# Sorting token numbers instead of token rows for the routed experts of a two-layer tower

## What is computed

```python
x = take(weight, idx)                         # 2048 rows of 256
x = x + LN(causal_linear_attention(LN(x)))    # layer 0, 16 heads, 16 tiles of 128 rows
x = x + ((LN(x) @ CB.T) * SCB / 127 + bias)
x = performer_block(LN(x), ...)               # layer 1: attention by 64 features, two matrices of 1024
logits = LN(x) @ router_w.T                   # 8 experts
top = argmax(logits); s = sigmoid(max(logits))
h = LN(x) * s                                 # the row that goes to its one expert
routed = (silu(h @ gate[top]) * (h @ up[top])) @ down[top]
shared = (silu(LN(x) @ sg) * (LN(x) @ su)) @ sd
out = x + shared + routed
```

## Time and profile before

| | |
|---|---|
| runs, us | 748.58, 749.82, 751.64; median 749.82 |
| profiled execution | 749.15 us, of it the span from the first to the last instruction 747.3 |
| mean granted TensorE clock | 0.970 |
| busy, share of the span | PE 91%, PEld 75%, DVE 64%, ACT 37%, POOL 27% |
| DMA | 69.81 MB, HBM read 28.74 MB, written 41.10 MB |
| chain that ended last | PE 83%, DVE 6%, issue 3%, the rest 8% |

### The profile page before, as it was taken

One profiled execution on the slowest core, in us unless ns is written; L12 is line 12 of the kernel. 1 busy time (PEld: TensorE's weight loads), 2 busy tenths in 40 slices (PEclk: granted clock), 3 DMA queues, 4 the chain that ended last, 5 costly groups with the idle time before them and its releaser, 6 DMA issues.

```text
span 747.3 us, 15335 instructions
## 1 busy us (share of the span) xinstructions
PE 679.7 (91%) x5738; PEld 563.1 (75%) x5739; DVE 481.6 (64%) x1185; ACT 277.1 (37%) x664; POOL 204.1 (27%) x379
## 2 busy tenths in 40 slices
PE   3838899999999999999999999999997399999995
PEld 2627788988889898989989898888886256565653
DVE  2549688887969788797988879777663422323231
ACT  1114443544344444534444453453442022222220
POOL 4632233313232422323242232422321011111111
PEclk9869999999999999999999999999999699999998
DMA  7999999999999500000000000000015411211110
GB/s 257 323 230 173 168 190 168 177 147 180 166 162 217 210 1 16 16 1 16 1 15 5 13 15 2 15 1 16 16 57 223 138 34 56 64 45 64 63 57 17
DMA packets 30911, 69.81 MB, mean 93 GB/s; under 512 B 3323, under 2 KB 9600, under 8 KB 29440
## 3 DMA queue, kind: packets, MB, share of 16 engines
q1 hardware_dynamic: 27696, 60.53, 37.0%
q0 software_dynamic: 3152, 8.40, 3.8%
HBM read 28.74 MB, written 41.10 MB: 93 GB/s over the span
## 4 chain that ended last, share of the span: by engine, by line
PE 83%; DVE 6%; issue 3%; ACT 2%; POOL 2%; DMA 2%; POOLq 0%; SPq 0%; DVEq 0%; ACTq 0%
PE ps L1030 76%; PE ps L1035 5%; PE ps L1199 2%; DMA H<-table,idx_sb 2%; POOL H L371 2%; ACT qkA L635 1%; DVE stats L659 1%; ACT yTB L625 1%; PE ps L1329 0%; POOL rstd L391 0%; DVE S_sb L725 0%; DMA yA<-sorted_rows 0%; DVE mv L660 0%; DVE kmax L811 0%; PE ps L1170 0%
## 5 line engine op out<-in xcount | busy, mean ns | idle before, releaser
L1030 PEld LDWEIGHTS ps<-yTC,we 128*128 128x128 f32 x1024 | 120.6, 194 | 6.5 <-issue 5.0
L1030 PE MATMUL ps<-yTC,we 128*128 128x128 f32 x1024 | 124.8, 279 | 0.5 <-ACT yTC L579 0.5
L390 POOL TENSOR_TENSOR var_eps<-mv,ln_eps 128x1 f32<-128x1 f32 x112 | 23.9, 213 | 370.4 <-DVE mv L660 370.1
L1030 PE MATMUL ps<-we,yTA 128*128 128x256 f32 (+1 forms) x288 | 97.1, 469 | 1.7 <-ACT yTB L625 1.4
L1030 PEld LDWEIGHTS ps<-we,yTA 128*128 128x128 f32 x288 | 54.6, 200 | 26.0 <-issue 20.9
L1030 PE MATMUL ps<-we,yTB 128*128 128x256 f32 (+1 forms) x216 | 73.1, 469 | 0.7 <-DVE yTB L863 0.6
L391 POOL TENSOR_TENSOR rstd<-var_eps,pow_half 128x1 f32<-128x1 f32 x112 | 66.4, 593 | 8.8
L1030 PE MATMUL ps<-we,ffT 128*128 128x256 f32 x256 | 61.3, 383 | 0.0
L1030 PEld LDWEIGHTS ps<-we,yTB 128*128 128x128 f32 x216 | 38.7, 191 | 23.7 <-issue 21.0
L1030 PEld LDWEIGHTS ps<-we,ffT 128*128 128x128 f32 x256 | 47.2, 190 | 5.6
L472 POOL DMA_INDIRECT out<-tmpA,home x12 | 11.8, 985 | 127.3 <-DVE tmpA L1019 127.3
(11 more groups left out here) (197 smaller groups left out, 1315.2 us busy)
## 6 DMA issues: line engine op xcount, KB each, us to landing
sorted_rows<-pads SPq DMA_DIRECT2D x16, 2052.0 KB, 49.1
we<-w_experts SPq DMA_DIRECT2D x8, 1536.0 KB, 19.5
home<-sorted_rows SPq DMA_DIRECT2D x23, 128.5 KB, 2.1
we<-w_ff SPq DMA_DIRECT2D x2, 1024.0 KB
rows_sb<-rows SPq DMA_DIRECT2D x1, 1664.0 KB, 7.0
yA<-sorted_rows SPq DMA_DIRECT2D x12, 128.0 KB, 2.1
yB<-sorted_rows SPq DMA_DIRECT2D x11, 128.0 KB, 2.1
we<-w_qk SPq DMA_DIRECT2D x2, 512.0 KB, 4.1
```

What stands on the lines that cost most here:

```text
L390: link(pool.tensor_tensor(var_eps[:, k:k + 1], mv[:, k, 1:2], ln_eps[:], ALU.add))
L1030: return pe.matmul(o, a, b, start=start, stop=stop)
```

## The change

The rows are no longer scattered. SP writes the scaled rows (`x_rows`) and the rows with the shared expert's part (`home_rows`) in token order by plain DMAs, with stages `x_out` and `home_out`. Only the tokens' numbers are scattered, 4 bytes each, into `sorted_ids`, which one write of out-of-bounds numbers clears beforehand; the 17 writes of padding rows go. When the table is there, SP loads for each of the 23 sorted tiles its column of 128 numbers (`load_ids`), each with a `value_load` and a DMA, two on one semaphore and 21 on another. The tiles are then fetched by these numbers with indirect DMAs that GpSimd issues (`fetch_x`, `fetch_home`); numbers out of bounds are left out.

The gathers from the table of rows are spread: three at the start, ahead of the constants' memsets, and one in each step behind r0 (`gat`), on four semaphores in turn. The table's instructions become stages `table0` to `table3` that run for the last tile only, behind `c_slot` and ahead of `c_down`; a masked sum takes the place of the prefix sum by doubling, and `tile_row` is made before `tile_expert`. The last expert's weights come in three parts as the shared expert's matmuls of the last tile finish, and PE waits for the down part only before the first down matmuls. The PSUM banks of the experts are dealt anew, so that the first gate and up matmuls do not write the bank of `c_dn`. Several waits of PE on a coming tile's semaphores are made only while there is such a tile. `yTC2` has six buffers, `gC` is gone, `home` lies in `ffT`, and the fetches and stores of GpSimd are written out instead of looped.

```diff
-GATHERED_ALONE = 3
+AHEAD = 6
+GATHERS = 4
...
-        send = sb("send", [P, ROW])
-        pads = sb("pads", [P, ROW])
-        home = [sb(f"home{s}", [P, D + 1]) for s in range(MOE_SLOTS)]
+        send_x, send_home = sb("send_x", [P, D]), sb("send_home", [P, D])
+        nowhere = sb("nowhere", [P, E * SPAN + 1], U32)
+        ids = sb("ids", [P, SORTED_TILES], U32)
...
+        x_rows = nc.dram_tensor("x_rows", [T * P, D], F32, kind="Internal").ap()
+        home_rows = nc.dram_tensor("home_rows", [T * P, D], F32, kind="Internal").ap()
+        sorted_ids = nc.dram_tensor("sorted_ids", [(E * SPAN + 1) * P, 1], U32, kind="Internal").ap()
...
-        banks_of = [[ps[:, 0, :], ps[:, 1, :], ps[:, 2, :], ps[:, 6, :]],
-                    [ps[:, 3, :], ps[:, 4, :], ps[:, 5, :], ps[:, 7, :]]]
+        banks_of = [[ps[:, 0, :], ps[:, 1, :], ps[:, 2, :], ps[:, 4, :]],
+                    [ps[:, 3, :], ps[:, 5, :], ps[:, 6, :], ps[:, 7, :]]]
...
-            sp.wait_ge(S["pads_ready"], 2)
-            sp.dma_start(sorted_dram[E * SPAN * P:, :], pads[:]).then_inc(rows_cleared[0], 16)
-            regions = sorted_dram[0:E * SPAN * P, :].rearrange("(e n p) r -> n p e r", e=E, p=P)
-            for n in range(T):
-                sp.dma_start(regions[n], pads[:].unsqueeze(1).broadcast_to([P, E, ROW])
-                             ).then_inc(rows_cleared[cleared_with(n)], 16)
+            sp.wait_ge(S["zero_ready"], 5)
+            sp.dma_start(sorted_ids.rearrange("(p n) one -> p (n one)", p=P), nowhere[:]).then_inc(S["ids_cleared"], 16)
...
-            sp.wait_ge(S["ffn0_psum"], T)
-            sp.wait_ge(S["out1_psum"], T)
-            load_experts(RESIDENT, freed_by_b, "experts_loaded")
-            sp.wait_ge(S["ff2_psum"], 2 * T)
-            load_experts(freed_by_b, freed_by_ff, "experts_loaded")
-            sp.wait_ge(S["down_psum"], T)
-            load_experts(freed_by_ff, E, "experts_loaded")
-
-            def first_row(j):
-                return sp.value_load(tile_row[0:1, bass.ds(j, 1)], min_val=0, max_val=E * SPAN * P)
-
-            def load(s, first):
...
+            def x_out(t):
+
+                sp.wait_ge(S["sent_ready"], t + 1)
+                sp.dma_start(x_rows[t * P:(t + 1) * P, :], send_x[:]).then_inc(S["x_kept"], 16)
+
+            def home_out(t):
+
+                sp.wait_ge(S["tile_done"], t + 1)
+                sp.dma_start(home_rows[t * P:(t + 1) * P, :], send_home[:]).then_inc(S["home_kept"], 16)
+
+            def free_b(t):
+
+                if t == T - 1:
+                    sp.wait_ge(S["ffn0_psum"], T)
+                    sp.wait_ge(S["out1_psum"], T)
+                    load_experts(RESIDENT, freed_by_b, "experts_loaded")
+
+            def free_ff(t):
+
+                if t == T - 1:
+                    sp.wait_ge(S["ff2_psum"], 2 * T)
+                    load_experts(freed_by_b, freed_by_ff, "experts_loaded")
+
+            last = we[:, freed_by_ff * EXPERT:E * EXPERT]
...
+            def load_ids(t):
+
+                if t < T - 1:
+                    return
+                sp.wait_ge(S["table_ready"], 1)
+                sp.wait_ge(S["ids_scattered"], 16 * T)
+                for j in range(SORTED_TILES):
+                    first = sp.value_load(tile_row[0:1, j:j + 1], min_val=0, max_val=E * SPAN * P)
+                    sp.dma_start(ids[:, j:j + 1], sorted_ids[bass.ds(first, P), :]
+                                 ).then_inc(S["ids_loaded0" if j < MOE_SLOTS else "ids_loaded1"], 16)
+
+            run_steps([
+                (2, home_out), (1, x_out), (0, free_b), (0, free_ff), (1, free_ga), (1, free_up), (1, free_dn),
+                (1, load_ids),
+            ])
...
+            def gather(t):
+
+                pool.indirect_dma_start(out=H[:, t, :], out_offset=None, in_=table,
+                                        in_offset=bass.IndirectOffsetOnAxis(ap=idx_sb[:, t:t + 1], axis=0)
+                                        ).then_inc(gathered[t % GATHERS], 16)
+
+            pool.wait_ge(S["idx_loaded"], 16)
+            for t in range(GATHERS - 1):
+                gather(t)
             pool.memset(proj_sb[:], 0.0).then_inc(S["zero_ready"], 1)
             pool.memset(hsum_sb[:], 0.0).then_inc(S["zero_ready"], 1)
-            pool.memset(pads[:], 0.0).then_inc(S["pads_ready"], 1)
+            pool.memset(nowhere[:], NOWHERE).then_inc(S["zero_ready"], 1)
...
+            def gat(t):
+
+                if t + GATHERS - 1 < T:
+                    pool.wait_ge(S["var0_ready"], t + 1)
+
+                    gather(t + GATHERS - 1)
+
             def pA(t):
 
                 if t == 0:
-                    for later in range(GATHERED_ALONE, T):
-                        gather(later, S["gathered_rest"])
-                    pool.wait_ge(S["vectors_loaded"], 16)
-                pool.wait_ge(gathered[t] if t < GATHERED_ALONE else S["gathered_rest"],
-                             16 if t < GATHERED_ALONE else 16 * (T - GATHERED_ALONE))
+                    pool.wait_ge(S["out0_loaded"], 16 * 3)
+                pool.wait_ge(gathered[t % GATHERS], 16 * (t // GATHERS + 1))
...
-                pool.wait_ge(rows_cleared[cleared_with(t)], 16 * (5, 6, T - 10)[cleared_with(t)])
-                pool.wait_ge(S["slot_ready"], t * 2 + 2)
-                pool.wait_ge(S["sent_ready"], t + 1)
-                pool.wait_ge(S["tile_done"], t + 1)
-                pool.indirect_dma_start(out=sorted_dram, in_=send[:], in_offset=None,
-                                        out_offset=bass.IndirectOffsetOnAxis(ap=slot_u[:], axis=0)
-                                        ).then_inc(S["scattered"], 16)
+                if t == 0:
+                    pool.wait_ge(S["ids_cleared"], 16)
+                pool.wait_ge(S["slot_ready"], t + 1)
+                pool.indirect_dma_start(out=sorted_ids, in_=tokens[:, t:t + 1], in_offset=None,
+                                        out_offset=bass.IndirectOffsetOnAxis(ap=slot_u[:, t:t + 1], axis=0)
+                                        ).then_inc(S["ids_scattered"], 16)
...
-                (0, r0), (3, pA2), (5, r4), (4, pB), (3, r3), (2, pA), (5, pC), (2, r1), (5, r5), (4, hC), (5, r6),
-                (2, r2), (6, scat),
+                (0, r0), (0, gat), (3, pA2), (5, r4), (4, pB), (3, r3), (2, pA), (5, pC), (2, r1), (5, r5), (4, hC),
+                (5, r6), (2, r2), (6, scat),
...
+            def fetch_x(i):
+
+                for s, j in tiles_of(i):
+                    if i > 0:
+                        pool.wait_ge(S["xT_psum"], j - (MOE_SLOTS - 1))
+                    pool.indirect_dma_start(out=xm[s], out_offset=None, in_=x_rows, in_offset=by_id(j),
+                                            bounds_check=T * P - 1, oob_is_err=False).then_inc(x_loaded[s], 16)
...
+            pool.wait_ge(S["ids_loaded0"], 16 * MOE_SLOTS)
+            pool.wait_ge(S["x_kept"], 16 * T)
+            fetch_x(0)
+            pool.wait_ge(S["ids_loaded1"], 16 * (SORTED_TILES - MOE_SLOTS))
+            fetch_x(1)
+            pool.wait_ge(S["home_kept"], 16 * T)
+            fetch_home(0)
+            for i in range(ROUNDS):
+                if i + 2 < ROUNDS:
+                    fetch_x(i + 2)
                 store(i)
-            store(ROUNDS - 1)
+                if i + 1 < ROUNDS:
+                    fetch_home(i + 1)
...
-                after(dve, "scattered", t * 16)
-                dve.tensor_copy(send[:, 2 * D:ROW].bitcast(U32), token[:]).then_inc(S["slot_ready"], 1)
-                dve.wait_ge(S["slot_ready"], t * 2 + 1)
-                link(dve.tensor_scalar(token[:], token[:], float(P), None, ALU.add))
-                dve.tensor_copy(slot_u[:], slot[:]).then_inc(S["slot_ready"], 1)
+                dve.tensor_copy(slot_u[:, t:t + 1], slot[:]).then_inc(S["slot_ready"], 1)
...
+            def table0(t):
+
+                if t < T - 1:
+                    return
+                link(dve.tensor_tensor(exceeds, base[:].unsqueeze(2).broadcast_to([P, E, T]), beyond[:], ALU.is_gt))
+                link(dve.tensor_reduce(need, exceeds, AX.X, ALU.add))
+                link(dve.tensor_tensor(summed, need.unsqueeze(1).broadcast_to([P, E, E]), up_to[:], ALU.mult))
+                link(dve.tensor_reduce(ends, summed, AX.X, ALU.add))
+
+            def table1(t):
+
+                if t < T - 1:
+                    return
+                link(dve.tensor_tensor(first_tile, ends, need, ALU.subtract))
...
+                link(dve.tensor_scalar(tile_row, sums, float(E * SPAN * P), None, ALU.add))
+                dve.sem_inc(S["table_ready"], 1)
...
+                (4, b_ks), (4, b_qs), (4, b_keps), (1, a_m2), (1, a_m3), (2, a_o), (1, a_m0), (6, c_slot),
+                (6, table0), (6, table1), (6, table2), (6, table3), (5, c_o), (1, a_m1), (2, a_res), (4, b_cx),
+                (5, c_res), (6, c_down),
...
-            pe.wait_ge(S["table_ready"], 1)
-            pe.wait_ge(S["experts_loaded"], 16 * E)
```

(46 more changed lines are left out.)

200 lines of the change are left out of this document (98 added, 102 removed).

## The result

The changed kernel takes 776.27 us (median of 4 runs, 773.47 to 778.81), the kernel before 749.2 us beside it. The ratio is 1.0374, its 95% interval 1.0339 to 1.041: slower by 27 us, where I had forecast no change. The profiled span is 777.0 us against 747.3; these 29.7 us are to be found.

A forecast was written before the change was run, and what follows sets the result against it. Both steady parts were taken as TensorE's, so time could move only in filling, first third and passage: -11.5 - 6.0 + 16.5 = -1.0 us on 749.15, 748.15, given as 748.5; range 738 to 757, the forecast's own 744 to 753.

The forecast's parts named there:

- Three DMAs in the place of one scatter, per tile: Tower steps: SP's two plain writes and GpSimd's scatter of numbers lie beside TensorE's 32.55 us a step, costing nothing.
- The scatter's landing: End of the tower: last small scatter leaves GpSimd at 582.3 and lands at 587.5, between 2.1 and 6.4 us.
- the passage: From tower to experts: +16.5 us, between +4.5 and +20, mostly from waiting for all the lists of numbers.
- The lists: Passage to experts: 23 list loads 1.15 us apart; round 1's second tile comes 14.9 us later, stalling round 0.
- Rival 3: Passage: list loads go one after another at a plain load's 2.1 us landing, 21 us more, 769; chance 0.04.
- The head: Filling of the tower: spreading the gathers removes two VectorE stalls, -11.5 us, between -9 and -13.
- The padding: Tower's first third: dropping the padding writes removes TensorE's issue gaps, 6 us gained (3.2 in steps), bounds 0 and 7.
- The gap at 84 us: Early tower: TensorE's 2.01 us issue gap, put down to full DMA engines, goes with the padding writes.
- the 2.9 us there: Early tower, at 84 us: padding gain of 2.0 for the gap and 0.9 for slow matmuls behind it.
- Rival 2: Tower's first third: issue gaps are not the padding's and stay, 754.2 us, slower; chance 0.12.
- The rounds: Expert part: the 12 rounds keep 12.23 us each, with the same matmuls.
- -1.0: Whole kernel: forecast sum of head, padding and passage in us, on the profiled execution's 749.15.

The follow-up runs named there:

- burst: Changed kernel with the 13 later gathers put back in one burst at the second step, none in the later steps: 787.2 us, ratio 1.0548.
- the gathers alone: Kernel before with only the 13 later table gathers spread one to a step, rows still scattered with padding: 736.63 us, ratio 0.9801; again on another chip 734.97 us.
- the wide spacing: Changed kernel with each number still written as 4 bytes, but the slots 64 bytes apart in memory: 755.21 us, ratio 1.0109.
- the extra drains: Mended changed kernel (737.89 us) plus a GpSimd drain behind the last scatter: 735.74 us; with three more ahead of stores of rounds 4, 8 and the last: 731.95 us.
- the lists by round: Changed kernel with list loads signalled separately for rounds 0, 1, 2 and the rest, last home rows written ahead of them: 761.42 us, ratio 1.0141.

## Why the prediction was wrong

**The step that failed** is the part "Three DMAs in the place of one scatter, per tile", and in it "All of it lies beside TensorE's 32.55 us a step". I looked for cover for GpSimd's and SP's time and asked nothing about the scatter's own. The changed kernel takes 421.04 us from the third to the sixteenth transposes, the one with 64-byte spacing 530.31 - 125.77 = 404.54: the stalls cost 16.5 us. Writing 4 bytes is not the cause (755.21 us with the same 4-byte writes), nor does it take a gather beside it (burst, 787.2); the 4-byte spacing is. How an engine is held is argued, not shown. ScalarE and VectorE stop together with no releaser in the program, TensorE behind ScalarE, and the instruction queue's packets take longer. In the trace's packet records 12 of the 43 of 16 KB last 2.0 to 5.2 us, against about 1.0 otherwise. One lies from 176.31 to 179.76, and the engines stand from 177.47 to 180.26; one from 276.04 to 279.38, and they stand from 277.02 to 280.57. The longest lies in the first stall but doesn't fit its end:

```profile
q8 instruction: 1, 0.02, 8.1%
```

This is the window from 140 to 144 us; 8.1% of 16 engines' 4 us is 5.2 us. The packet starts at 140.80 and ends at 146.0, and ScalarE goes on at 143.61. Nine of the 12 have no stall of the chain over 1.5 us beside them, and the stall at 349.29 has no long packet. Much of this fits engines which wait for their next instructions, but it doesn't prove it. The Trainium skill's "Runtime: NRT & Kernel Launch", section "Instruction fetch mechanics", calls crossing such a block "mostly hidden". The stalls of up to 5.9 us don't agree with it for these kernels, if that is what they are.

**The scatter's landing**, bounded by 2.1 and 6.4 us and taken near 5, measured 8.28 in the passage with 4-byte spacing and 4.20 with 64 bytes. Bounds from a plain load and from a scatter of whole rows did not hold for one of 4-byte neighbours. It put SP's begin about 3 us further behind `slot_u` than I had.

**The lists** went as written. They are 25.2 / 22 = 1.14 us apart (1.15 forecast), round 0's down matmuls waited behind transpose_x(1), and the clock fell a second time. With a quick scatter the passage to the second tile costs 601.99 - 530.31 = 71.7 us, 15.3 more than before (14.9 forecast). In the kernel after it is 20.6 more. Of the 5.3 us between the two, the scatter's landing is 8.28 - 4.20 = 4.1; the scatter also left 1.6 us later behind the sixteenth transposes (35.26 against 33.68), for which I have no cause, and the lists were 0.4 quicker. Rival 3, one landing after another, did not happen. The rule behind it, to coalesce (the Trainium skill, "DMA: Bandwidth & Descriptors", section "Rules for kernel authors"), points the right way, but the 46 us of its fixed costs in a row did not show: the 23 loads took 25.5 us, 1.14 apart, with a landing of 1.97 for the last, so SP's issue sets the pace.

**The head** gave 11.5 us in the kernel with the gathers alone, and 11.6 here; tile 3's statistics stand at 36.61 (36 forecast). That the numbers agree so closely is in part luck: the kernel with the gathers alone was profiled twice, and its third transposes stand at 129.40 in one execution and at 124.68 in the other. **The padding** gave the 3.2 us of the steps (407.73 to 404.54). The gap at 84 us is gone, but TensorE waits 2.07 us for VectorE until 80.82 with a dip of the clock behind it (granted clock 0.65, then 0.50); the kernels with this start and no padding vary from 125.09 to 129.34 at the third transposes, so the 2.9 us there are unclear. Rival 2 falls: neither the chain of this kernel nor that of the wide spacing has such an "issue" gap behind 60 us in the tower.

**Two terms were missing.** The rounds: two more waits, 0.1 us a round, where I had written 12.23 unchanged. With 13.53 us for the round behind the stall (1.3 more than 12.23, where I had taken 1.6 for slow down matmuls) and a last block of down matmuls that takes 3.07 us, before 1.99, they make most of the 3.7 us. The end: 101 indirect DMAs on GpSimd instead of 55 lengthen its last drain from 5.78 to 9.56 us.

So from -1.0 to +29.7: 16.5 of stalls, 20.55 + 3.65 - 16.5 = 7.7 in the passage and rounds, 3.8 in the drain, and 2.7 of padding in the head that didn't come; together 30.7.

What stays open: what the engines wait for; whether spacings between 4 and 64 bytes would do; why only some steps stall; and how much the extra drains would give the kernel before.

## What to carry to other kernels

Before a wide, orderly transfer is replaced by a scatter of small elements, price the scatter's landing and its effect on every other queue, not only its issue: slots 4 bytes apart cost this kernel 21 us against slots 64 bytes apart, and spacing them is one multiplication. Where one count of a semaphore covers loads that are needed at different times, the first consumer waits for the last load. A change that adds indirect DMAs to GpSimd adds to its drain at the end; a drain can be put where that engine is idle.

## What the runs showed of the hardware

- 128 numbers of 4 bytes scattered to slots 4 bytes apart landed in 8.28, 8.65 and 9.56 us (the last scatter of the kernel after, of the burst and of the lists by round), at 64-byte spacing in 4.20, all beside the expert loads. With 64-byte rows the last one landed in 4.49 us, and the median of the 16 is 2.2. Widening the rows to 512 bytes gained nothing (756.48 against 755.3; the last one landed in 4.30). The Trainium skill's "DMA: Bandwidth & Descriptors", section "Specifications", says that below 512 bytes the engine does a read-modify-write. A penalty that lasts up to 512 bytes doesn't show here; one for writes 4 bytes apart does.
- Beside and behind such scatters other packets took longer. In the kernel after, 93 of the 192 packets of 4096 bytes that the gathers moved from 120 us on lasted over 1 us, up to 6.7, and 12 of 43 instruction packets over 2 us, up to 5.2; at 64-byte spacing all of them stayed under 0.5 and 1.5. ScalarE, VectorE and TensorE stood still for up to 5.9, 4.9 and 4.1 us.
- GpSimd's last drain took 5.78 us behind 55 indirect DMAs, 6.93 behind 69 and 9.56 behind 101: 0.082 us each and 1.26 beside. Behind a single one it took 2.43, up to that one's landing.
- Two waits that are long satisfied, in TensorE's loop over the rounds, took 0.1 us a round (12.34 against 12.23).
